# Perceiver block on one core: the gate softmax of the mixture of experts behind the first expert's first layer, the bias product one expert later, and 24 idle products on TensorE

## What is computed

```python
def _L1_ffn_ref(x, W1, b1, W2, b2, W3, b3, Wg, bg):
    NE, TOPK = 8, 2
    gate_logits = jnp.einsum('bsd,dn->bsn', x, Wg) + bg
    gate_weights = jax.nn.softmax(gate_logits, axis=-1)
    topv, topi = jax.lax.top_k(gate_weights, TOPK)
    h = jax.nn.gelu(jnp.einsum('bsd,ndh->nbsh', x, W1) + b1[:, None, None, :], approximate=False)
    h = jax.nn.gelu(jnp.einsum('nbsh,nhf->nbsf', h, W2) + b2[:, None, None, :], approximate=False)
    eo = jnp.einsum('nbsf,nfd->nbsd', h, W3) + b3[:, None, None, :]
    comb = jnp.sum(jax.nn.one_hot(topi, NE, dtype=x.dtype) * topv[..., None], axis=-2)
    return jnp.einsum('nbsd,bsn->bsd', eo, comb)
# x = x + _L1_ffn_ref(_layernorm(x), ...)
```

## Time and profile before

| | before |
|---|---|
| three runs, us | 490.94, 493.5, 493.93 |
| median, us | 493.5 |
| the profiled execution, us | 491.93 |
| its span in the profile, us | 490.1 |
| TensorE matmul busy | 418.6 us, 85% |
| DVE busy | 334.4 us, 68% |
| ACT busy | 267.0 us, 54% |
| POOL busy | 110.0 us, 22% |

### The profile page before, as it was taken

One profiled execution on the slowest core, in us unless ns is written; L12 is line 12 of the kernel. 1 busy time (PEld: TensorE's weight loads), 2 busy tenths in 40 slices (PEclk: granted clock), 3 DMA queues, 4 the chain that ended last, 5 costly groups with the idle time before them and its releaser, 6 DMA issues.

```text
span 490.1 us, 9082 instructions
## 1 busy us (share of the span) xinstructions
PE 418.6 (85%) x3628; PEld 307.4 (63%) x3628; DVE 334.4 (68%) x537; ACT 267.0 (54%) x594; POOL 110.0 (22%) x88
## 2 busy tenths in 40 slices
PE   0168789998978898998998889996999799999997
PEld 0115556665645586486444624445889689999996
DVE  3788766678568977894366654865554788877872
ACT  4405887776758717431233315556771286777762
POOL 3002346001294010000022352233000203333300
PEclk9999999999989999999999979998899799999999
DMA  6599186543751078137200000019300595540000
GB/s 226 130 256 277 25 202 174 141 120 90 185 197 48 3 235 305 44 123 297 95 1 1 0 3 0 1 45 361 109 2 0 168 346 175 172 172 1 1 2 23
DMA packets 25002, 58.28 MB, mean 119 GB/s; under 512 B 5209, under 2 KB 13689, under 8 KB 21114
## 3 DMA queue, kind: packets, MB, share of 16 engines
q1 hardware_dynamic: 24960, 57.69, 37.2%
HBM read 44.77 MB, written 0.29 MB: 92 GB/s over the span
## 4 chain that ended last, share of the span: by engine, by line
PE 63%; DVE 18%; ACT 7%; issue 6%; POOL 2%; DMA 2%; SPq 0%; ACTq 0%; DVEq 0%; POOLq 0%
PE ps L1289 19%; PE ps L1093 9%; PE ps L924 7%; PE ps L911 5%; PE ps L880 4%; DVE mx L1666 3%; ACT reg_b L683 3%; PE ps L959 2%; PE ps L1254 2%; PE ps L1244 2%; PE ps L1243 2%; PE ps L1003 2%; POOL qreg L472 2%; PE ps L1090 1%; DMA x<-in_x 1%
## 5 line engine op out<-in xcount | busy, mean ns | idle before, releaser
L1666 DVE TENSOR_REDUCE mx<-ps 128x1 f32<-128x1024 f32 x64 | 77.0, 1221 | 36.5 <-PE ps L880 24.9
L683 ACT ACTIVATE reg_b<-ps 128x512 f32<-128x512 f32 x128 | 74.9, 598 | 26.6 <-PE ps L911 17.2
L911 PE MATMUL ps<-qreg,reg_b 98*128 98x128 bf16 x512 | 47.3, 225 | 5.7 <-ACT reg_b L683 4.2
L1093 PE MATMUL ps<-reg_b,xT 128*128 128x512 f32 x96 | 49.8, 643 | 0.0
L1289 PE MATMUL ps<-part_a 128*128 128x256 f32 x384 | 48.2, 283 | 0.4 <-DVE part_a L1819 0.4
L911 PEld LDWEIGHTS ps<-qreg,reg_b 98*128 98x128 bf16 x512 | 35.2, 100 | 19.8 <-ACT reg_b L683 9.7
L1289 PEld LDWEIGHTS ps<-part_a 128*128 128x128 f32 x384 | 46.9, 192 | 0.6 <-DVE part_a L1819 0.6
L396 POOL TENSOR_TENSOR rstd<-ve,cf 128x1 f32<-128x1 f32 x12 | 6.8, 567 | 174.0 <-DVE ve L1362 174.0
L822 ACT ACTIVATE reg_a<-ps,b 128x256 f32<-128x256 f32 x64 | 30.2, 472 | 24.4 <-PE ps L1289 24.4
L924 PE MATMUL ps<-reg_b 128*32 128x128 f32 x1024 | 43.0, 285 | 0.3 <-ACT reg_b L683 0.3
L880 PE MATMUL ps<-reg_b,qreg 96*128 96x512 bf16 x96 | 34.3, 427 | 10.2 <-DMA reg_b<-reg_b 7.5
(11 more groups left out here) (279 smaller groups left out, 849.1 us busy)
## 6 DMA issues: line engine op xcount, KB each, us to landing
reg_b<-in_w SPq DMA_DIRECT2D x16, 512.0 KB, 7.6
reg_b<-in_w SPq DMA_DIRECT2D x8, 1024.0 KB, 7.3
reg_b<-reg_b SPq DMA_DIRECT2D x56, 128.0 KB, 3.2
reg_b<-in_w_qkv SPq DMA_DIRECT2D x3, 2048.0 KB, 7.5
reg_b<-reg_a SPq DMA_DIRECT2D x40, 128.0 KB, 3.2
reg_a<-in_ctxK SPq DMA_DIRECT2D x4, 1024.0 KB, 7.5
reg_a<-in_ctx SPq DMA_DIRECT2D x8, 512.0 KB, 4.7
reg_b<-bc_mem SPq DMA_DIRECT2D x4, 1024.0 KB, 6.6
```

The costliest lines, as they stand in the source:

```text
L683: sc.activation(pT[n % 3], score_b[n % 2], ACT.Exp).then_inc(S("exp_done"), 1)
L911: mm = pe.matmul(cols, kS[g % 3][0:SROWS, c // 8, j, P * (c % 8):P * (c % 8 + 1)], qT[b][0:SROWS, HPG * hg + j, :], start=not last, stop=True)
L1093: mm = pe.matmul(bank(b, n % 2), xT[b][:, i, :], w_qkv[j][:, i, 512 * n:512 * (n + 1)], start=False, stop=i == KD - 1)
L1666: ve.reduce_max(mx[:, piece // 2, piece % 2:piece % 2 + 1], score_a[m % 2].rearrange("p i k -> p (i k)"), X_AXIS).then_inc(S("max_done"), 1)
```

## The change

Five edits:

1. PE issues `keep_busy(7, 24)` between the two transposes `x_to_columns(5, 0)` and `x_to_columns(5, 1)`, ahead of the wait for `x_done1`.
2. ACT's two gate exponentials move from ahead of `hidden(0, 0)` to behind it and behind the rounding of W2 of expert 1. The program now has a table load for Gelu ahead of the first layer, one for the exponential, and one back to Gelu.
3. DVE's `gate_weights(0)` and `gate_weights(1)` move from behind `lower_hidden(0, 0)` to behind `lower_hidden(0, 1)`.
4. DVE's `lower_weights(0, 2)` moves from ahead of `lower_hidden(0, 0)` to behind it.
5. The transposes of `comb` move from behind `hidden2(0)` to behind `hidden2(1)`; the copy of `combT` and the product with `b3` with its addition move one expert later. `add_expert(0)` waits for `comb_done`.

```diff
+            def gate_exp(b):
                 sc.wait_ge(S("g_shift"), b + 1)
                 sc.activation(comb[b][:, :], logit[b][:, 0:NE], ACT.Exp, accum_out=small[b][:, 2:3])\
                     .then_inc(S("g_exp"), 1)
...
+                if e == 0:
+                    for b in range(NB):
+                        gate_exp(b)
                 hidden(e, 1)
-                if e == 0:
+                if e == 1:
                     sc.wait_ge(S("combT_ps"), 1)
...
             for b in range(NB):
+                if b == 1:
+                    keep_busy(7, 24)
                 pe.wait_ge(S(f"x_done{b}"), 5)
                 x_to_columns(5, b)
...
                 hidden1(e)
-                if e == 1:
+                if e == 2:
                     pe.wait_ge(S("combT_sb"), 1)
...
                 hidden2(e)
-                if e == 0:
+                if e == 1:
                     for b in range(NB):
                         pe.wait_ge(S("comb_done"), b + 1)
...
             lower_weights(0, 1)
-            lower_weights(0, 2)
...
+                    if e == 0:
+                        ve.wait_ge(S("comb_done"), b + 1)
...
                 lower_hidden(e, 0)
                 if e == 0:
-                    for b in range(NB):
-                        gate_weights(b)
+                    lower_weights(0, 2)
                 if e + 1 < NE:
                     lower_weights(e + 1, 0)
                     lower_weights(e + 1, 1)
-                if e == 1:
+                if e == 2:
                     for b in range(NB):
                         ve.wait_ge(S("b3_ps"), b + 1)
+                        ve.wait_ge(S("eo_added"), b + 1)
                         link(ve.tensor_tensor(x[b][:, :], ps[:, b, 0:D], x[b][:, :], ALU.add))
                 if e >= 1:
                     add_expert(e - 1)
                 lower_hidden(e, 1)
+                if e == 0:
+                    for b in range(NB):
+                        gate_weights(b)
                 if e + 1 < NE:
                     lower_weights(e + 1, 2)
```

## The result

| | before | changed |
|---|---|---|
| first measurement, us | 492.42 (490.94 to 493.93, 4 runs) | 498.96 (496.54 to 499.39, 4 runs) |
| ratio to before | | 1.0124, interval 1.0094 to 1.0154 |
| again, beside 29 runs of before, us | 492.07 (488.83 to 496.29) | 497.55 (496.64 to 499.92, 6 runs) |
| ratio to before | | 1.0119, interval 1.0079 to 1.0159 |
| the profiled execution, its span, us | 491.93, 490.1 | 498.77, 497.0 |

The change makes the kernel slower by 1.2%, 5.5 to 6.5 us. 496.4 us with a range to 498.5 was forecast, +2.9 on a median of 493.5; the first median lies above that range. The new wait is where the prediction put it and as long; of the gain that was to pay for a part of it, the part that the 24 idle products were to bring did not come.

What follows compares the result with a forecast made beforehand. PE's uninterrupted expert matmuls were taken to bound the kernel. -2.7 at the start, +0.4 on ACT, a pause taking the remaining 2.3 and 1.4 more, and 1.5 for the clock gave +2.9 on 493.5: 496.4 us, range 491.5 to 498.5.

Steps and rivals of the forecast that it cites:

- The new wait: PE ahead of hidden2(1), waiting for DVE's first low part of the second expert behind both gates: a 3.7 us pause.
- What bounds the kernel: PE's uninterrupted run of 648 expert matmuls from 405.51: whatever moves its start moves the end by the same amount.
- The start, 2.7 us won: From 383 us: idle products keep the clock full, first Gelu earlier; last low part at 393.7 instead of 396.4.
- The middle on ACT: Between expert 0's layers: W2 rounding, two loads, exponentials; hidden(0, 1) at 398.3, expert_out(0) at 401.9, leaving 2.3 us won.
- no drain shows: Rival: a drain with each ACT table load, as long as the load, 2.6 us more, 499.0; chance 0.02.
- the middle of the bounds, 1.1: POOL's two instructions meeting DVE's last gate operations, lower_weights(1, 2) and first low part: bounds 0 and 2.1 us, 1.1 taken.
- The clock behind it: Behind the new pause, 3.4 us at half clock under dense matmuls, costing 1.5 us.
- The rival with half clock twice as long: Half clock lasts twice as long behind the new pause: +1.4 + 3.0, 497.9 us; chance 0.06.
- The sum: -2.7 at the start, +0.4 on ACT, pause taking 2.3 and 1.4 more, 1.5 for clock: +2.9, 496.4 us.
- the break-even of 407.1: The moment PE must go on with hidden2(1) for no loss; forecast 408.5, 1.4 us later.
- The range: 491.5 to 498.5 us; slower by over 1% was given 0.10.
- idle products in vain: Rival: idle products don't hold the clock, nothing won at the start; first low part at 409.2, +4.7, 498.2; chance 0.10.

Runs made afterwards that it cites:

- e2: The changed kernel without the 24 idle products: 499.29 us, ratio 1.0135 to the kernel before.
- e7: The changed kernel with 27 idle products instead of 24, 2 more ahead of the gate's product and 6 ahead of hidden1(0): 497.67 us, ratio 1.0084.
- e1: The changed kernel with both of DVE's gate_weights moved further back, behind lower_hidden(1, 0): 494.03 us, ratio 1.0025 to the kernel before.
- e4: The changed kernel with POOL's rounding of W3 of expert 2 held until DVE has all four low parts of expert 1's first layer: 496.37 us, ratio 1.0059.
- e6: The changed kernel with ACT's gate exponentials back ahead of the first Gelu: 496.27 us, ratio 1.0081 to the kernel before.
- e8: The changed kernel with the gate (ACT's exponentials, DVE's gate_weights, comb's transposes, product with b3) one expert later: 492.30 us, ratio 0.9999.
- e11: The changed kernel with only one gate_weights, that of batch 1, moved behind lower_hidden(1, 0): 494.91 us, ratio 1.0044.
- e3: The kernel before with the 24 idle products alone: 491.37 us, ratio 0.9982.
- e9: As e8, with 27 idle products instead of 24, 2 ahead of the gate's product and 6 ahead of hidden1(0): 491.58 us, ratio 0.9991.
- e12: As e1, with the further idle products of e9: 490.96 us, ratio 0.9979 to the kernel before.

## Why the prediction was wrong

All times of the changed kernel less 2.29 us, the later start of its stage.

- **What bounds the kernel**: right. From 423.86 on PE runs through, and the end moved by what PE lost ahead of it.
- **The start, 2.7 us won**: the step that failed. "They should keep the clock full" held to 391.5 (389.2 in this count), in the middle of what it was meant for; `hidden1(0)` then ran at half clock, 18 matmuls in 3.94 us. The last k-step of the first tile went on at 397.42 - 2.29 = 395.1 instead of 393.7, 1.3 us won instead of 2.7. On ACT, whose way leads to the new wait, the rounding of W2 began at 396.81 - 2.29 = 394.5 instead of 393.15. Counted from the start of the stage that is 13.87 us (13.62 in the repetition); without the idle products (e2) it is 13.87 too, so in these profiles they did next to nothing. With more of them (e7) it is 12.56, where the prediction has 393.15 - 380.65 = 12.50, and the stage is 1.1 us shorter: the sum was right, its premise of full clock was not. The clock fell in `hidden1(0)` in all seven profiles of changed kernels with 24 idle products (the two of the change, e1, e4, e6, e8, e11), and stayed full in e3; what decides it is open.
- **The middle on ACT**: right but for that delay. From the rounding of W2 to the first Gelu of the second layer it is 401.84 - 396.81 = 5.03 us, 5.15 was forecast, and no drain shows. `expert_out(0)` starts at 403.3 instead of 401.9.
- **The new wait**: right in place and mechanism, 3.73 us long where 3.7 was forecast. Both of its ends are 1.6 later than forecast, so that the close match of the length is in part luck: the end has 0.3 of it from a longer collision. With POOL held, first gate operation to first low part is 405.40 to 410.71, 5.31 us; in the changed kernel 405.56 to 412.25, 6.69. So the collision cost 1.4 and not the middle of the bounds, 1.1.
- **The clock behind it**: right. 48 matmuls took 7.34 instead of 5.76 us: 1.6 for a forecast 1.5. The rival with half clock twice as long was a real one: in e2 they took 8.71, 2.95 us lost.
- **The sum**: PE goes on at 412.38 - 2.29 = 410.1, 3.0 behind the break-even of 407.1 instead of 1.4, and with 1.6 for the clock it is +4.6 instead of +2.9. Of the missing 1.7, 1.3 are the start, 0.3 the collision and 0.1 the clock.
- **The range**: it ended at 498.5, and gave slower by over 1% a tenth. On the 493.5 of the forecast, +4.6 makes 498.1, inside it; the first median lay beyond, since it is 6.5 above a median of before of 492.42, of which the stage holds 4.4 to 5.3. One program's executions lie 7 us apart, and the range left no room for that. The rival "idle products in vain", +4.7, came nearest: its condition, that the products don't hold the clock, held, and it had PE go on at 409.2 + 1.1 = 410.3, measured 410.1. It had been given a tenth.

## What to carry to other kernels

When work is moved off an engine's critical place, add up the row of work between its new place and the next instruction that another engine waits for: 2.1 us of slack don't hold 3.8 us of gate, however small its operations are, and a stage that is made faster ahead of it eats the slack too. Moving it by one more step cost the stage nothing (e1). Idle products that fill a pause are not sure to hold the clock: where they covered the thin work behind it as well, it stayed full in three profiles of three (e7, e9, e12), where they filled the pause alone in one of eight (e3). Whether they did anything is read from the same kernel without them (e2).

## What the runs showed of the hardware

- Half clock doesn't need a long pause: in e11 it came behind three waits of PE of 0.5 to 0.6 us, 1.5 together, with three matmuls between them. And a long one doesn't always bring it at once: behind 3.03 us the clock stood at half from 387 in the kernel before, but was full until 387 in e2, where the pause ended at 385.35, and fell in `hidden1(0)` only.
- Whether a short pause brings half clock differs between executions of one program: behind the 2.13 us ahead of 57 us it was full once and half once, which alone cost 2.5 us. The same place of the program was reached 4.7 us apart. A single pair of profiles is to be compared from the first changed instruction on, not by the span.
- A DVE operation of 8 elements, 0.17 us by itself (e4), took 0.94 beside a POOL rounding of 1024 elements (changed kernel); four of 256 elements took 3.10 (e11) instead of 1.42 beside two such roundings.
